# A graph layer on one core: the node 1/sqrt of four blocks at once by seed and Newton steps on VectorE, one-hots in pairs, and another order at the end of the binning

## The reference

```python
h = jnp.maximum(_layernorm(x, axis=-1), 0.0)          # (x - m) / sqrt(v + 1e-5)
s, v = h[:, :64], h[:, 64:].reshape(N, 32, 3)
skip_s, skip_v = s @ W_skip0, einsum('nmi,mk->nki', v, W_skip1)
xs, xv = (s @ W_nl0)[dst], (v by W_nl1)[dst]
w = relu(edge_feature @ W_fc1) @ W_fc2                 # 224 weights an edge
tp = products of w, xs, xv and the unit edge vector    # dot, cross, scaled
agg = segment_sum(tp, src, num_segments=N) / 32
out_s, out_v = agg_s @ W_out_s + skip_s, agg_v by W_out_v + skip_v
return x + concat([silu(out_s[:, :64]), sigmoid(out_s[:, 64:])[:, :, None] * out_v])
```

## Time and profile before

| | us |
|---|---|
| median of 3 runs | 1369.47 (1368.71 to 1371.86) |
| profiled execution, its own time | 1372.43 |
| span of its records | 1370.6 |
| PE, DVE, ACT, POOL busy | 1213.3, 1214.9, 1004.9, 983.2 |
| TensorE's mean granted clock | 0.978 of full speed |

### The profile page before, as it was taken

The page is one execution under the profiler, slowest core; times in us unless marked ns, Lnnn a source line. Parts: engine busy times, 40 slices in busy tenths (PEclk is TensorE's granted clock), DMA queues, the critical chain, the costliest instruction groups (busy, mean ns, idle before and its releaser), DMA issues.

```text
span 1370.6 us, 33958 instructions
## 1 busy us (share of the span) xinstructions
PE 1213.3 (89%) x8857; PEld 995.2 (73%) x8857; DVE 1214.9 (89%) x4487; ACT 1004.9 (73%) x2379; POOL 983.2 (72%) x1135
## 2 busy tenths in 40 slices
PE   4999968999999999986888888888888888888886
PEld 2455537888888888875777777777777777777775
DVE  7999967888889888766999999999999999999996
ACT  3999966788888888855777777767677777767774
POOL 4333347788778888517888888888888888888883
PEclk9999988999999999998999999999999999999998
DMA  3000002344443444325787878778787778878774
GB/s 108 1 0 0 0 20 63 106 112 111 108 112 109 113 109 110 98 69 135 221 238 224 230 229 228 227 226 242 213 240 223 234 225 229 232 224 239 225 230 131
DMA packets 90920, 212.27 MB, mean 155 GB/s; under 512 B 15030, under 2 KB 56281, under 8 KB 90878
## 3 DMA queue, kind: packets, MB, share of 16 engines
q1 hardware_dynamic: 62462, 155.23, 35.9%
q0 software_dynamic: 28416, 56.56, 18.3%
HBM read 127.73 MB, written 84.00 MB: 154 GB/s over the span
## 4 chain that ended last, share of the span: by engine, by line
POOL 42%; PE 29%; issue 17%; DVE 7%; ACT 2%; DMA 1%; DVEq 1%; POOLq 0%; ACTq 0%; SPq 0%
POOL mg L565 32%; POOL n_rstd L571 8%; PE bank L1161 5%; PE bank L1098 4%; PE bank L1214 3%; PE bank L1190 3%; PE bank L1178 3%; PE bank L1145 2%; PE bank L1174 2%; PE bank L1176 2%; DVE rank_junk L717 2%; PE bank L1198 2%; ACT hn L962 2%; DVE bin_hot L681 1%; PE bank L1218 1%
## 5 line engine op out<-in xcount | busy, mean ns | idle before, releaser
L565 POOL DMA_INDIRECT mg<-messages,slot_m x392 | 453.6, 1157 | 121.1 <-issue 110.0
L1035 ACT ACTIVATE nn<-xb,n_bias,n_rstd 128x160 f32<-128x160 f32 x588 | 299.5, 650 | 111.3 <-DVE n_bias L662 109.8
L1240 PE MATMUL bank<-wsk_a,nt_a 128*128 128x160 f32 x1568 | 298.4, 313 | 55.0 <-DVE ob L845 53.2
L1240 PEld LDWEIGHTS bank<-wsk_a,nt_a 128*128 128x128 f32 x1568 | 226.7, 192 | 75.9 <-issue 52.0
L498 POOL DMA_INDIRECT xg<-x,dst_g x200 | 208.2, 1041 | 62.3 <-issue 57.1
L1042 ACT ACTIVATE nt_a<-bank 128x512 f32<-128x512 f32 x196 | 117.0, 597 | 105.8 <-PE bank L1233 105.8
L1254 PE MATMUL bank<-mg,hot 64*128 64x192 f32 x1568 | 181.2, 350 | 11.7 <-DVE hot L832 11.7
L644 DVE BATCH_NORM_STATS2 n_stat<-xb 128x6 f32<-128x160 f32 x784 | 186.7, 312 | 3.7 <-DMA xb<-x 3.4
L1232 PE MATMUL bank<-ident,nn 128*128 128x128 f32 x784 | 147.5, 311 | 35.2 <-ACT nn L1035 30.0
L1232 PEld LDWEIGHTS bank<-ident,nn 128*128 128x128 f32 x784 | 110.2, 210 | 91.6 <-issue 54.0
L571 POOL TENSOR_TENSOR n_rstd<-n_sum,neg_half 128x8 f32<-128x8 f32 x98 | 163.7, 1670 | 12.7 <-DVE n_sum L658 10.6
(11 more groups left out here) (172 smaller groups left out, 2724.4 us busy)
## 6 DMA issues: line engine op xcount, KB each, us to landing
xb<-x SPq DMA_DIRECT2D x97, 640.0 KB, 5.9
out_dram<-ob SPq DMA_DIRECT2D x97, 640.0 KB, 3.5
messages<-msg SPq DMA_DIRECT2D x50, 390.6 KB
mg<-messages,slot_m POOLq DMA_INDIRECT x392
ef<-edge_feat_t SPq DMA_DIRECT2D x50, 125.0 KB, 5.9
xg<-x,dst_g POOLq DMA_INDIRECT x200
xb<-x SPq DMA_DIRECT2D x1, 420.0 KB
out_dram<-ob SPq DMA_DIRECT2D x1, 420.0 KB
```

The source lines that it names most:

```text
L565: pool.indirect_dma_start(mg[:, u, k, :], None, messages[:, :], bass.IndirectOffsetOnAxis(ap=slot_m[:, u, k:k + 1], axis=0)).then_inc(n.g[ ...
L1035: last = act.activation(nn[:, u % 2, h, :, g % 4], xb[:, u, g, :], ACT.Relu, bias=n_bias[:, u, g:g + 1], scale=n_rstd[:, u, g:g + 1])
L1240: pe.matmul(z[:, t, 0:F], nt_a[:, h, t * P:(t + 1) * P], wsk_a[:], start=(t % 2 == 0), stop=False, skip_group_check=True)
```

## The change

Node stage. `ln_n` and GpSimd's `pow` are gone; GpSimd keeps the fetches alone. VectorE computes the 1/sqrt for four blocks together (32 columns instead of 8): a seed by an integer shift and a subtraction, and three Newton steps, in one round of four, spread between its other work. The `bn_stats` of such a group of four (32 of them) are spread over the other three rounds, 10, 11 and 11. The ring of x has eight buffers, loaded seven ahead. The four one-hots of a block become two `tensor_tensor` of 128x256. The loop of rounds is unrolled by eight instead of four. The opening of the node stage is spread over three rounds at the end of the edges, and ScalarE's part of it stands one round later.

Binning. Of each five tiles GpSimd makes the last one's `slot_v` itself, with one `tensor_scalar` after its seven small instructions; ScalarE makes four. The products of zeros are gone. TensorE begins with the edges behind `b_free` (three VectorE instructions after the last table product) instead of `b_fin`. The rest of the list `slots_i` and of the largest counts is moved into VectorE's round 0 of the edges (`table()`), and the edge vectors and output weights are done between the last rank and the wait for the tables.

```diff
-        U = 4
+        U, XU = 4, 8
+        AHEAD = (10, 21)
+        SEED = 1597463007.0
@@ gpsimd, tile_b, after the slots of five tiles
+                        r = k % BLOCK
+                        wait(pool, b_tab, t - BLOCK + 1)
+                        pool.wait_ge(b_dec, n + 1)
+                        pool.tensor_scalar(slot_v[:, r, :], iota_slot[0:ET, :], slot[:, k:k + 1], row_no[:, r:r + 1],
+                                           ALU.is_equal, ALU.mult).then_inc(b_last, 1)
@@ gpsimd, nodes
-                    def ln_n(i, u):
-                        pool.wait_ge(n.var, i + 1)
-                        pool.tensor_tensor(n_rstd[:, u, :], n_sum[:, u, 4, :], neg_half[:, :], ALU.pow).then_inc(n.pw, 1)
@@ vector, behind the last tile of the binning
-                dve.wait_ge(b_end, 1)
-                (whole, most, rest, empty, tab_row, slots_i: L733 to L752)
+                dve.wait_ge(s_sqrt, 1)
+                (vec_r, vec_n, hat, wo_s, wo_u, wo_v: moved here from behind the list)
+                dve.wait_ge(b_tab, NT)
+                dve.tensor_scalar(whole[:], p_cnt[(NT - 1) % 2], 1.0 / W_EVEN, None, ALU.mult).then_inc(b_free, 1)
                 dve.wait_ge(b_rows_sb, 1)
+                for r in range(2):
+                    dve.scalar_tensor_tensor(out=empty[:, r, :], in0=p_tab[r], scalar=0.0, in1=empty[:, r, :],
+                                             op0=ALU.is_gt, op1=ALU.mult).then_inc(b_free, 1)
+                def table():
+                    (13 instructions: tab_row, slots_i, most; the last one gives b_fin)
@@ vector, round_e
+                    if isinstance(q, int) and q == 0:
+                        table()
                     if isinstance(q, int) and q == NG:
+                        nodes(main, False, (FIRST,))
+                    if isinstance(q, int) and q == NG + 1:
+                        nodes(main, False, (SECOND,))
+                    if isinstance(q, int) and q == NG + 2:
                         nodes(main, False, (OPEN,))
@@ vector, nodes
+                    def halve(i, u):
+                        dve.tensor_scalar(n_seed[:, b, :], n_sum[:, b, 4, :].bitcast(I32), 1, None,
+                                          ALU.logical_shift_right).then_inc(n.root, 1)
+                    def seed(i, u):
+                        dve.tensor_scalar(n_rstd[:, b, :].bitcast(I32), n_seed[:, b, :], -1.0, SEED, ALU.mult,
+                                          ALU.add).then_inc(n.root, 2)
+                    def root_a(i, u, k):
+                        dve.wait_ge(n.root, base + 7)
+                        dve.tensor_tensor(n_step[:, b, 0, :], y, y, ALU.mult).then_inc(n.root, 1)
+                    def root_b(i, u, k):
+                        dve.wait_ge(n.root, base + 8)
+                        dve.scalar_tensor_tensor(out=n_step[:, b, 1, :], in0=n_step[:, b, 0, :], scalar=-0.5,
+                                                 in1=n_sum[:, b, 4, :], op0=ALU.mult, op1=ALU.mult).then_inc(n.root, 1)
+                    def root_c(i, u, k):
+                        dve.wait_ge(n.root, base + 9)
+                        dve.scalar_tensor_tensor(out=y, in0=n_step[:, b, 1, :], scalar=1.5, in1=y,
+                                                 op0=ALU.add, op1=ALU.mult).then_inc(n.root, 1)
-                        for k in bins:
-                            last = dve.tensor_scalar(hot[:, u % 2, k, :], iota_local[:], mg[:, u, k, LOCAL:LOCAL + 1],
-                                                     None, ALU.is_equal)
+                        bins = slice(2 * half, 2 * half + 2)
+                        made = dve.tensor_tensor(hot[:, u % 2, bins, :], iota_local[:].unsqueeze(1).to_broadcast((P, 2, P)),
+                                                 mg[:, m, bins, LOCAL:LOCAL + 1].to_broadcast((P, 2, P)), ALU.is_equal)
+                        if u % U == 3 and macro_exists(i + 5):
+                            stats_n(i + 5, (u + 5) % XU, 0, AHEAD[0])
+                        if u % U == 0 and macro_exists(i + 4):
+                            stats_n(i + 4, (u + 4) % XU, AHEAD[0], AHEAD[1])
+                        if u % U == 1 and macro_exists(i + 3):
+                            stats_n(i + 3, (u + 3) % XU, AHEAD[1], U * G)
@@ scalar, tile_b
+                    if k % BATCH < BATCH - 1:
                         (off_slot and slot_v as before)
-                act.wait_ge(b_end, 1)
+                act.wait_ge(b_tab, NT)
@@ tensor
-                for o in (*p_cnt, *p_tab):
-                    last = pe.matmul(o, zeros_h[...], zeros_h[...], start=False, stop=True, skip_group_check=True)
-                last.then_inc(b_end, 1)
-                pe.wait_ge(b_fin, 1)
+                pe.wait_ge(b_free, 3)
```

More of the change, by code:

```diff
@@ L279, in __init__ @@
                 self.st = [sem(f"{name}_st{u}") for u in range(U)]
-        OPEN, ROUNDS = "open", "rounds"
+        FIRST, SECOND, OPEN, ROUNDS = "first", "second", "open", "rounds"
         main = Nodes("n")
@@ L582, in round_n @@
                     def round_n(i, u):
-                        if macro_exists(i + 2):
-                            if not every:
-                                fetch(i + 2, (u + 2) % U)
-                            ln_n(i + 2, (u + 2) % U)
+                        if macro_exists(i + 2) and not every:
+                            fetch(i + 2, (u + 2) % XU)
                     macros(pool, round_n)
@@ L594, in _ @@
                 pool.wait_ge(e_st[1], 16 * (NG // 2))
[L595 removed]
+                nodes(main, False)
                 pool.wait_ge(b_fin, 1)
@@ new lines, in _ @@
+                dve.tensor_scalar(wo_u[V:2 * V, :], wo_u[V:2 * V, :], 1.5 ** 0.5 / 32.0, None, ALU.mult)
+                for j in range(2):
+                    same, cross = slice(2 * V * j, 2 * V * j + V), slice(2 * V * j + V, 2 * V * j + 2 * V)
+                    dve.tensor_scalar(wo_v[same, :], wo_v[same, :], 1.0 / 32.0, None, ALU.mult)
+                    last = dve.tensor_scalar(wo_v[cross, :], wo_v[cross, :], 1.5 ** 0.5 / 32.0, None, ALU.mult)
+                last.then_inc(s_wready, 1)
@@ L745, in _ @@
-                for r in range(2):
-                    last = dve.scalar_tensor_tensor(out=tab_row[:, r, :], in0=empty[:, r, :], scalar=2.0 * BLOCK * ET,
-                                                    in1=tab_row[:, r, :], op0=ALU.mult, op1=ALU.add)
-                link(last)
-                dve.tensor_tensor(most[:, 3:4], most[:, 0:1], most[:, 2:3], ALU.max)
-                link(dve.tensor_tensor(empty[:, 0, :], tab_row[:, 0, :], tab_row[:, 1, :], ALU.add))
-                dve.tensor_copy(most_i[:], most[:, 3:4])
@@ L892, in nodes @@
                     if not every:
-                        hot_n(0, 0)
+                        hot_n(0, 0, 0)
+                        hot_n(0, 0, 1)
                     def round_n(i, u):
+                        before, after = (u + 7) % XU, (u + 1) % XU
+                        j, w = i + 2, (u + 2) % XU
+                        extract = u % U == 2 and macro_exists(j)
                         if macro_exists(i - 1):
-                            gate(i - 1, (u + 3) % U, 1)
+                            gate(i - 1, before, 1)
@@ L898, in round_n @@
+                        if extract:
+                            spread(j, w)
                         if macro_exists(i + 1):
-                            shift_n(i + 1, (u + 1) % U)
-                            norm_last(i + 1, (u + 1) % U)
+                            norm_last(i + 1, after)
+                        if extract:
+                            squares(j, w)
                         if macro_exists(i - 1):
-                            residual(i - 1, (u + 3) % U)
+                            residual(i - 1, before)
@@ L903, in round_n @@
+                        if extract:
+                            variance(j, w)
                         if macro_exists(i + 1) and not every:
[L904 to L912 removed]
+                            hot_n(i + 1, after, 0)
+                            if extract:
+                                halve(j, w)
+                            hot_n(i + 1, after, 1)
+                        elif extract:
+                            halve(j, w)
@@ L1117, in tile_b @@
                     pe.wait_ge(b_rank, t + 1)
-                    count(k, tri_rest, k)
+                    count(k, tri_rest, k, not tile_exists(t + 2))
                     if tile_exists(t + 2):
@@ L1253, in add @@
                             pair = 2 * h + t % 2
-                            last = pe.matmul(q_z[h][:, t, 0:Z], hot[slots, u % 2, pair, :], mg[slots, u, pair, 0:Z],
+                            last = pe.matmul(q_z[h][:, t, 0:Z], hot[slots, u % 2, pair, :], mg[slots, u % U, pair, 0:Z],
                                              start=False, stop=True, skip_group_check=True)
```

327 lines of the change are left out of this document (191 added, 136 removed).

## The result

| | before | after |
|---|---|---|
| median | 1369.2 (1368.71 to 1371.86, 4 runs) | 1291.25 (1290.25 to 1293.93, 4 runs) |
| ratio | | 0.9416, 95% interval 0.9400 to 0.9431 |
| profiled execution, its own time | 1372.43 | 1290.25 |
| span | 1370.6 | 1288.4 |

78 us less; 1301.5 was predicted, so the gain came out 10.25 us larger than forecast.

What follows compares the result with a forecast made beforehand. GpSimd's round was taken to bound the nodes, over half the span. Gains of 61.5 in the nodes and 9.4 at the binning's end, less 3 in its loop, gave 67.9: 1304.5 profiled, 1301.5 us median, range 1288 to 1314.

Steps and rivals of the forecast that it cites:

- The bound: Nodes: GpSimd's seamless round of power and four fetches, 7.49 us, is the limit; the other engines wait for it.
- VectorE's sum: Nodes after the change: VectorE's work adds up to 27.2 us for four rounds, 6.79 a round; 6.87 taken.
- kept work: Nodes, VectorE: norm_last 0.55, residual 1.40 and two gates 1.58 stay, 3.53 us a round.
- the 18 small ones: Nodes, VectorE: 18 instructions of 32 columns per four blocks, nine at 0.22 and nine at 0.11, cost 3.0 us, raised to 3.1.
- 0.06 for waits: Nodes: allowance a round on top of VectorE's sum for waits from uneven rounds, giving 6.87 us.
- The rule against pairing: Nodes: by elements alone, the skill's rule has paired one-hots lose 0.27 us a round; the prediction took a 0.12 gain.
- Binning, loop: Binning loop: GpSimd's new instruction, 0.3 to 0.4 us, 40 times, may hold up VectorE; 3 us lost, bounds 0 and 16.
- Binning, end: End of binning: TensorE starts the edges near 196.0 instead of 203.61, 7.4 us less; 9.4 taken with the second transposes.
- The second transposes' wait: Start of edges: TensorE's 2.08 us wait for rows whose bias stood behind the edge vectors goes.
- The list of rows: Edges, round 0: 13 VectorE instructions of about 5 us fill a round without products; up to 5 if uncovered.
- Opening of the nodes: Opening of the nodes: 16 statistics ahead of the last two message blocks; counted 0, within 3.7 us either way.
- Rival 1: Nodes: close limits interlock, uneven VectorE rounds delay TensorE; round of 7.15, gain 34.9, 1328 us; chance 0.20.

Runs made afterwards that it cites:

- e8: Changed kernel with each of the 18 small statistics and Newton instructions of four blocks cut into four of 128x8; 1385.61 us, ratio 1.0113 to before.
- e9: Changed kernel without TensorE's skip products of the last 32 features in the node stage; 1293.53 us, ratio 0.944 to before.
- e1: Changed kernel with two Newton steps instead of three for the node 1/sqrt; 1471.5 us on a slower chip.
- e4: Changed kernel without VectorE's addition of x to the output (8 of 1280 columns still added); 1567.37 us on a slower chip.
- e5: Changed kernel with two Newton steps instead of three, run a second time; 1473.18 us on a slower chip.
- e3: Changed kernel with a block's one-hots as four tensor_scalar of 128x128 instead of two tensor_tensor of 128x256; 1467.78 us on a slower chip.
- e7: Changed kernel with GpSimd's slot one-hot given back to ScalarE, which makes all five of five tiles; 1477.26 us on a slower chip.
- e10: Kernel before with only the new binning (GpSimd's one-hot and the new order at its end), nodes as before; 1360.53 us, ratio 0.9924.
- a0: Changed kernel unchanged, run on a slower chip; 1466.75 us, ratio 1.0064 to before.

## Why the prediction was right, and where it was off

**The bound.** Right. GpSimd was the limit, and behind it VectorE: it is the new engine of the chain, 98.49 of 100. e8 shows that work added to it is added to the round, and e9 that TensorE's 6.5 was not the limit; that work taken from VectorE would shorten the round no run shows, since e1, e4 and e5 fell on slower chips.

**VectorE's sum.** 27.2 for four rounds was forecast and 27.18 measured (6.74 + 6.47 + 6.70 + 7.27 from residual to residual). By term: kept work 3.53 a round, the same; one-hots 0.66, measured 0.67; statistics 7.3, measured 7.27 (2.27 + 2.50 + 2.50); the 18 small ones 3.0 raised to 3.1, measured 3.08, with 0.225 a dependent step. From gate to gate 5.98, 7.80, 6.70, 6.70, as listed. What failed is the last line: 0.06 for waits and 0.02 for the branch were put on top, and neither came (6.785 against 6.87). The 0.25 of slack in the 6.7 rounds was enough. That is 95 x 0.085 = 8.1 us, the largest single miss.

**The rule against pairing.** The 0.27 a round by elements alone did not come; e3 shows 0.11 the other way. The prediction put it down to the fixed part of an instruction, which would outweigh slower elements. By the rows under e3 only half of that is so: there were no slower elements, since the `tensor_scalar` one-hot took as long (0.196) as a `tensor_tensor` of its size (0.202), and about 0.06 a pair saved is all of the gain.

**Binning, loop.** 3 forecast, 1.0 to 1.2 measured. GpSimd's new instruction was mis-sized: 0.83 us (828 ns mean of 40), not 0.3 to 0.4, because it was priced by a product of two inputs. That the step still came out small shows that its length is not what VectorE pays: 33 us of GpSimd work beside a full VectorE cost one. The Trainium skill, "SBUF — State Buffer", section "Who interferes with whom", has a GpSimd instruction and a VectorE one in a two-port mode exclude each other for the whole instruction. These profiles show no such hold for this pair (0.03 us beside an instruction of 0.83); whether VectorE's one-hot is in such a mode no run shows.

**Binning, end.** 7.4 forecast, 7.46 measured from the last rank; e7 and e10 confirm both parts of it. The second transposes' wait went as said. The list of rows took its 5 us (4.75) in round 0 (198.97 to 203.72), where the prediction called it hidden. It was, but for 0.7: `products(0)` began at 205.60, without idle time ahead, though TensorE's projection for it was done at 204.87. TensorE waited 1.92 for `tp` behind it instead of 0.93, and there its clock fell. It doesn't show in the sum, because before lost 3.65 in the same way three rounds later, in the execution that was profiled. The 3.0 taken off as its distance from the median may in part be this one event, which the comparison with e8 to e10 puts at 1.7 to 2.0; no trace of another execution shows it.

**Opening of the nodes.** 0 forecast within 3.7; 1.1 gained.

**The sum.** 61.5 + 9.4 - 3 = 67.9 against 69.6 + 12.9 - 0.3 = 82.2: 8.1 more in the nodes and 6.5 ahead of them: 3.4 the loop (the 3 that were forecast, and 0.44 by which this execution's last rank even was earlier), 0.2 the end, 0.8 the third transposes, 1.0 between the two clock falls, 1.1 the opening. Of these 14.3 some 4 belong to the two profiled executions and not to the medians, which leaves the 10.

**What would show it.** GpSimd waits about 0.5 us a round for TensorE (52.7 us in all), not over 1: its fetches grew from 1157 to 1245 ns on average. The DMA share is 0.89, not 0.85. The new GpSimd instruction took 0.83, not 0.3 to 0.4, and ScalarE's wait for the bias came once, not in one round of four. The other marks came.

**The chances.** Rival 1, with 0.20, didn't come on a chip like the one predicted for. On three other chips rounds even longer than its 7.15 did (7.81 in a0), with a TensorE that seems to lag in place of uneven rounds; none of the rivals had that, nor does the profile that the prediction was made from show it. There the forecast would have been wrong; that the result came from a chip of the faster kind was luck.

## What to carry to other kernels

When an engine's small instructions are the cost, group the data and not only the code: 18 instructions of 32 columns cost 3.08 us where 72 of 8 columns cost 6.9, and the change turned from a gain of 78 to a loss of 14 with nothing else different. This holds for VectorE; GpSimd's power costs 0.16 us for each column more, so grouping saves little there. Add up what is next in line from distances between starts, term by term: here the sum was exact to 0.1%, and the allowance for waits on top was the error, so ask for a wait by name before allowing for it.

## What the runs showed of the hardware

- GpSimd's `tensor_scalar` of 125x128 in f16 with two operations takes 0.81 to 0.99 us, twice its product of 125x128 in f32 (0.41), yet costs the full VectorE beside it about 0.03 each (bin one-hots of 406 ns beside it, 377 elsewhere; after).
- A `tensor_scalar` one-hot of 128x128 in f32, with a column of scalars, takes 0.196 us from start to start, as long as a `tensor_tensor` of 128 columns (0.202); with constants in place of the column, 200 columns took 0.27 beside 0.37.
- TensorE's clock fell to 1.2 GHz behind a single wait of 1.79 us in otherwise full edges (before), and behind waits of 0.47, 0.81 and 1.92 (after). A wait of that length doesn't decide it alone: e8's nodes have one of 1.9 us in every fourth round, and its clock stayed at 2.4 GHz through them from 709 to 985 us and from 1176 to 1378, and fell at each of the seven between.
- One chip is not another: the same kernel before took 1371 and 1456 us, and what was a gain of 5.7% on one was a loss of 0.6% on the other. The time is lost where TensorE is nearly always busy; why is open.
